# Shared network as eight items of one-pass products, expert outputs parked in gathered rows, router by token tiles

## What is computed

```python
logits = jnp.einsum('bsd,ed->bse', hidden_states, gate_w)
scores = jax.nn.softmax(logits, axis=-1).transpose(0, 2, 1)
topk_w, topk_idx = jax.lax.top_k(scores, cap)
x_tok = jnp.take_along_axis(hidden_states[:, None, :, :], topk_idx[..., None], axis=2)
g = jnp.einsum('becd,efd->becf', x_tok, Wg)
u = jnp.einsum('becd,efd->becf', x_tok, Wu)
h = jax.nn.gelu(g, approximate=False) * u
eo = jnp.einsum('becf,edf->becd', h, Wd) * topk_w[..., None]
flat = flat.at[flat_idx].add(eo.reshape(-1, d))
gs = jnp.einsum('bsd,fd->bsf', hidden_states, Ws_g)
us = jnp.einsum('bsd,fd->bsf', hidden_states, Ws_u)
shared = jnp.einsum('bsf,df->bsd', jax.nn.gelu(gs, approximate=False) * us, Ws_d)
```

## Time and profile before

| what | value |
|---|---|
| median of 3 runs | 706.13 us (705.79 to 706.93) |
| profiled execution | 705.49 us |
| its span, first to last instruction | 703.7 us |
| PE busy | 669.1 us, 95% |
| DVE, ACT, POOL busy | 287.4, 240.2, 34.1 us |
| share of PE in the chain that ended last | 81% |
| granted PE clock, mean | 0.995 |
| expert stage, from the first expert's gate product | 424.8 us on |

### The profile page before, as it was taken

The page is one execution under the profiler, slowest core; times in us unless marked ns, Lnnn a source line. Parts: engine busy times, 40 slices in busy tenths (PEclk is TensorE's granted clock), DMA queues, the critical chain, the costliest instruction groups (busy, mean ns, idle before and its releaser), DMA issues.

```text
span 703.7 us, 10425 instructions
## 1 busy us (share of the span) xinstructions
PE 669.1 (95%) x4272; PEld 427.7 (61%) x4272; DVE 287.4 (41%) x603; ACT 240.2 (34%) x468; POOL 34.1 (5%) x35
## 2 busy tenths in 40 slices
PE   6989999999999999799989789999999999999996
PEld 5767778787777875488966563444444444444532
DVE  5964544636454264766775552111111111111112
ACT  4744545545354452556771131111111111111110
POOL 0300000000000000570000100000000000000000
PEclk9999999999999999999999999999999999999999
DMA  8111011010700000303097704899999999999911
GB/s 306 69 61 61 20 42 61 1 61 2 299 1 2 1 1 2 105 3 129 1 378 278 300 0 141 343 403 373 411 358 391 385 372 383 366 402 373 383 46 61
DMA packets 14348, 129.69 MB, mean 184 GB/s; under 512 B 2720, under 2 KB 2848, under 8 KB 6240
## 3 DMA queue, kind: packets, MB, share of 16 engines
q1 hardware_dynamic: 12384, 127.09, 46.5%
q10 hardware_dynamic: 1920, 1.97, 0.9%
HBM read 126.03 MB, written 1.05 MB: 181 GB/s over the span
## 4 chain that ended last, share of the span: by engine, by line
PE 81%; DVE 10%; ACT 4%; issue 1%; DMA 1%; SPq 1%; ACTq 1%; DVEq 0%
PE ps L969 21%; PE ps L1227 15%; PE ps L1259 8%; PE ps L1234 7%; PE ps L1266 4%; PE ps L1148 4%; PE ps L1039 4%; PE ps L1015 2%; PE ps L1050 2%; PE ps L1248 2%; PE ps L1080 2%; PE ps L1185 2%; PE ps L1197 1%; DVE stats L636 1%; PE ps L1114 1%
## 5 line engine op out<-in xcount | busy, mean ns | idle before, releaser
L865 DVE TENSOR_TENSOR hid<-hid,ps 128x256 f32<-128x256 f32 (+1 forms) x32 | 17.6, 553 | 141.3 <-PE ps L1227 91.4
L579 ACT ACTIVATE hid<-ps 128x256 f32<-128x256 f32 (+1 forms) x32 | 15.7, 490 | 141.6 <-PE ps L1234 86.5
L1259 PE MATMUL ps<-w_d,hid_T 128*64 128x512 f32 x256 | 58.4, 598 | 1.3 <-ACT hid_T L594 1.3
L1227 PE MATMUL ps<-w_u,x_slot 128*64 128x512 f32 x256 | 58.4, 598 | 0.0
L1227 PE MATMUL ps<-w_g,x_slot 128*64 128x512 f32 x256 | 57.8, 594 | 0.0
L465 ACT ACTIVATE probs<-ps,neg_max 128x512 f32<-128x512 f32 x64 | 43.5, 687 | 39.1 <-DVE neg_max L716 39.1
L969 PE MATMUL ps<-wv_hi,ctx_hi 128*128 128x512 f32 x128 | 51.6, 403 | 0.0
L696 DVE COPY probs_T<-ps 128x512 f32<-128x512 f32 x32 | 22.1, 691 | 68.7 <-PE ps L1039 68.7
L969 PE MATMUL ps<-wv_lo,ctx_hi 128*128 128x512 f32 x128 | 50.1, 392 | 0.0
L969 PE MATMUL ps<-wv_hi,ctx_lo 128*128 128x512 f32 x128 | 49.9, 390 | 0.0
L716 DVE TENSOR_REDUCE neg_max<-ps 128x1 f32<-128x512 f32 x64 | 39.7, 683 | 18.4 <-PE ps L1015 18.3
(11 more groups left out here) (192 smaller groups left out, 1145.8 us busy)
## 6 DMA issues: line engine op xcount, KB each, us to landing
w_u<-in_wu SPq DMA_DIRECT2D x16, 2048.0 KB, 15.9
w_d<-in_wd SPq DMA_DIRECT2D x16, 2048.0 KB, 13.9
w_g<-in_wg SPq DMA_DIRECT2D x16, 2048.0 KB, 9.6
ctx_raw<-in_ctx SPq DMA_DIRECT2D x7, 1024.0 KB, 4.7
w_qkv<-in_wqkv SPq DMA_DIRECT2D x1, 3072.0 KB, 15.2
ws_g<-in_wsg SPq DMA_DIRECT2D x1, 2048.0 KB, 7.9
ws_u<-in_wsu SPq DMA_DIRECT2D x1, 2048.0 KB, 8.0
ws_d<-in_wsd SPq DMA_DIRECT2D x1, 2048.0 KB, 21.3
```

The source lines that it names most:

```text
L865: dve.tensor_tensor(hid[:, n % 2, 0:w], hid[:, n % 2, 0:w], ps[:, 2 * (n % 2) + 1, 0:w], ALU.mult).then_inc(hid_done, 1)
L1227: ins = pe.matmul(ps[64 * fh:64 * (fh + 1), dst, :], x_slot[:, dt, e, :], weights[e % 2][:, dt, BANK * fh:BANK * (fh + 1)], start=(dt == 0 ...
L1259: ins = pe.matmul(ps[64 * fh:64 * (fh + 1), 6 + n % 2, :], hid_T[:, n % 2, j, 64 * fh:64 * (fh + 1)], w_d[e % 2][:, KT * fh + j, :], start ...
```

## The change

**Shared network.** Instead of 16 quarters there are eight items. Item i has 128 of the hidden columns and all 512 tokens. Weights, normalised rows and hidden rows are each split in a high part in the one-pass form and the rest, and a product is the sum of three one-pass products (high by high, high by low, low by high). Gate and value products come out as [hidden, token], so no transposes follow; the down products go tile by tile over two pairs of banks. `shared_high_gu`, `shared_high_d` (ScalarE) and `shared_low_gu`, `shared_low_d`, `hidden_low` (VectorE) make the parts. One item stands ahead of the experts, one after each of the experts 1, 3, ... 13.

**Outputs.** `eo_slot` now lies over the shared gate weights, so the rows of batch b can be written only after shared item b. Experts' outputs are parked in their gathered rows in `x_slot`, and `send` puts out what has come free.

**Layer norm and router.** Transposes and copies go by token tiles; VectorE's part (`xn_low_tile`) for tile t-1 stands in the middle of tile t's norm. The router's products have three one-pass parts of 32 columns.

**Start of the stage.** The routing tables lie in the second `w_d` buffer, so the load of w_d for expert 1 waits for their last reader. The broadcast of the scores moves behind the second expert's value product.

```diff
+        eo_slot = sb(first, "eo_slot", [P, B, D])
...
+        ws_g_lo = sb(first, "ws_g_lo", [P, NF, KT, P], F32R)
+        ws_u_lo = sb(first, "ws_u_lo", [P, NF, KT, P], F32R)
...
+        ws_g = sb(moe, "ws_g", [P, NF, KT, P])
+        ws_u = sb(moe, "ws_u", [P, NF, KT, P])
...
-        x_slot = sb(moe, "x_slot", [P, KT, E, SLOTS])
+        x_slot = sb(moe, "x_slot", [P, E, KT, SLOTS])
...
-        SHARED = [("s", t, q * QUARTER, QUARTER) for t in range(NT) for q in range(4)]
-        ITEMS, REST = SHARED[:2], SHARED[2:]
+        SHARED = [("s", i) for i in range(NF)]
+        ITEMS, REST = SHARED[:1], SHARED[1:]
         for e in range(E):
             ITEMS.append(("e", e))
-            for _ in range(2 if e == E - 3 else 1 if 0 < e < E - 3 else 0):
+            if e % 2 and REST:
                 ITEMS.append(REST.pop(0))
         AT = {item: n for n, item in enumerate(ITEMS)}
...
+        def experts_upto(n):
+            return n + 1 - shared_before(n + 1)
+
+        def downs_upto(n):
+
+            return experts_upto(n) + NT * shared_before(n + 1)
+
+        def shared_down_bank(n, t):
+            return (4, 6)[t % 2] + n % 2
...
-            for kind in "gud":
-                expert_load(kind, 1)
+            expert_load("g", 1)
+            expert_load("u", 1)
             for e in range(2, E, 2):
-                for kind, ahead in (("g", 0), ("u", 0), ("g", 1), ("d", 0), ("u", 1), ("d", 1)):
+                for kind, ahead in (("g", 0), ("u", 0), ("g", 1)):
+                    expert_load(kind, e + ahead)
+                if e == 2:
+                    sp.wait_ge(give_ps, 2)
+                    sp.wait_ge(last_T_done, NT)
+                    expert_load("d", 1)
+                for kind, ahead in (("d", 0), ("u", 1), ("d", 1)):
                     expert_load(kind, e + ahead)
...
+            def shared_high_gu(i):
+
+                if i:
+                    act.wait_ge(g_ps, AT["s", i - 1] + 1)
+                    act.wait_ge(u_ps, AT["s", i - 1] + 1)
+                act.copy(ws_g_hi[:], ws_g[:, i]).then_inc(ws_hi_done, 1)
+                act.copy(ws_u_hi[:], ws_u[:, i]).then_inc(ws_hi_done, 1)
+
+            def shared_high_d(i):
+                if i:
+                    act.wait_ge(down_ps, downs_upto(AT["s", i - 1]))
+                act.copy(ws_d_hi[:], ws_d[:, i, :]).then_inc(ws_hi_done, 1)
+
...
+            for t in range(NT):
+                ln_std(2, (t,))
+                if t:
+                    xn_high_tile(t - 1)
+            xn_high_tile(NT - 1)
...
             def send(n):
...
+                ready, free = experts_upto(n - 1), shared_before(n + 1)
+                was_ready, was_free = experts_upto(n - 2), shared_before(n)
+                for e in range(ready):
+                    if e >= was_ready:
+                        act.wait_ge(eo_done, e + 1)
+                    for b in range(0 if e >= was_ready else was_free, free):
+                        row = SLOTS * (e % 2) + CAP * b
+                        act.dma_start(eo_slot[CAP * e:CAP * (e + 1), b, :], eo_of(e)[row:row + CAP, :]).then_inc(eo_sent[e % 2], 16)
...
+                if is_expert(n):
+                    act.wait_ge(hidT_ps, experts_upto(n))
+                    act.copy(hid_T[:, n % 2].rearrange("p j c -> p (j c)"), bank(4 + n % 2)).then_inc(hidT_done, 1)
+                else:
+                    act.wait_ge(hid_done, n + 1)
+                    act.copy(hid_hi[:, n % 2, :], hid[:, n % 2, :]).then_inc(hid_hi_done, 1)
+                if 1 < n < LAST:
+                    send(n)
...
-                elif ITEMS[n][0] == "e":
+                elif is_expert(n):
                     e = ITEMS[n][1]
-                    act.wait_ge(down_ps, n + 1)
-                    if e >= 2:
-                        act.wait_ge(eo_sent[e % 2], 16 * B * (e // 2))
+                    act.wait_ge(down_ps, downs_upto(n))
                     mine, other = eo_rows(e)
-                    act.copy(eo[mine, :], ps[other, 6 + n % 2, :]).then_inc(half_done, 1)
+                    act.copy(eo_of(e)[mine, :], ps[other, 6 + n % 2, :]).then_inc(half_done, 1)
...
+                earlier = ITEMS[n - 2]
+                split_next = earlier[0] == "s" and earlier[1] + 1 < NF
+                if split_next:
+                    shared_high_gu(earlier[1] + 1)
                 item_out(n - 1)
+                if split_next:
+                    shared_high_d(earlier[1] + 1)
             item_out(LAST - 1)
-            send(LAST - 1)
+            send(LAST)
...
+                    if behind and t:
+                        behind(t - 1)
                     ln_rows(k, t, xn)
...
+                if behind:
+                    behind(NT - 1)
+
+            def xn_low_tile(t):
+                toks = slice(P * t, P * (t + 1))
+                dve.wait_ge(xn_hi_done, 2 * KT + t + 1)
+                dve.tensor_tensor(xn_lo_moe[:, :, toks], bank(t).rearrange("p (k c) -> p k c", k=KT),
+                                  xn_hi[:, :, toks].bitcast(F32), ALU.subtract).then_inc(xn_split, 1)
...
+            dve.tensor_tensor(gate_lo[:], gate[:], gate_hi[:].bitcast(F32), ALU.subtract).then_inc(gate_split, 1)
+            shared_low_gu(0)
+            shared_low_d(0)
+            residual_ln(2, xn_moe, xn_low_tile)
...
+            def hidden_low(n):
+
+                dve.wait_ge(hid_hi_done, shared_before(n) + 1)
+                dve.tensor_tensor(hid_lo[:, n % 2, :], hid[:, n % 2, :], hid_hi[:, n % 2, :].bitcast(F32),
+                                  ALU.subtract).then_inc(hid_split, 1)
...
+                        dve.wait_ge(sx_done, NT * shared_before(n))
+                    for t in range(NT):
+                        dve.wait_ge(down_ps, downs_upto(n) - NT + t + 1)
+                        dve.tensor_tensor(x[:, t, :], bank(shared_down_bank(n, t)), x[:, t, :], ALU.add).then_inc(sx_done, 1)
...
+            for n in range(3, LAST):
+                if not is_expert(n - 1):
+                    hidden_low(n - 1)
+                earlier = ITEMS[n - 2]
+                split_next = earlier[0] == "s" and earlier[1] + 1 < NF
+                if split_next:
+                    shared_low_gu(earlier[1] + 1)
                 item_hidden(n)
                 item_sum(n - 1)
+                if split_next:
+                    shared_low_d(earlier[1] + 1)
...
+            def moe_transpose(t):
+                pe.wait_ge(xn_done, 2 * NT + t + 1)
+                for dt in range(KT):
+                    ins = pe.transpose(ps[:, t, P * dt:P * (dt + 1)], xn_moe[:, t, P * dt:P * (dt + 1)], ident[:])
+                ins.then_inc(xnT_ps, 1)
+
...
+            for t in range(NT):
+                moe_transpose(t)
...
+                    i = ITEMS[n][1]
+                    hi, lo = shared_parts
+                    pe.wait_ge(ws_split, 3 * i + off + 1)
+                    for dt in steps:
+                        w_hi_part, w_lo_part = hi[:, dt, :], lo[:, i, dt, :]
+                        for j, (a, c) in enumerate(((w_hi_part, xn_hi), (w_hi_part, xn_lo_moe), (w_lo_part, xn_hi))):
+                            ins = pe.matmul(bank(dst), a, c[:, dt, :], start=(dt == 0 and j == 0),
+                                            stop=(dt == KT - 1 and j == 2))
...
+                    i = ITEMS[n][1]
+                    pe.wait_ge(ws_split, 3 * i + 3)
+                    pe.wait_ge(hid_split, shared_before(n) + 1)
+                    for t in range(NT):
+                        if t >= 2:
+                            pe.wait_ge(sx_done, NT * shared_before(n) + t - 1)
+                        rows = slice(P * t, P * (t + 1))
+                        for j, (a, c) in enumerate(((hid_hi, ws_d_hi[:]), (hid_lo, ws_d_hi[:]), (hid_hi, ws_d_lo[:, i, :]))):
+                            ins = pe.matmul(bank(shared_down_bank(n, t)), a[:, n % 2, rows], c, start=(j == 0), stop=(j == 2))
+                        ins.then_inc(down_ps, 1)
...
             for t in range(NT):
+                toks = slice(P * t, P * (t + 1))
+                pe.wait_ge(xn_split, 2 * KT + t + 1)
                 for dt in range(KT):
-                    ins = pe.matmul(ps[:, 6, LGW * t:LGW * (t + 1)], xn_T[:, dt, P * t:P * (t + 1)], gate[:, dt, :],
-                                    start=(dt == 0), stop=(dt == KT - 1))
+                    for j, (a, c) in enumerate(((xn_hi, gate_hi), (xn_hi, gate_lo), (xn_lo_moe, gate_hi))):
+                        ins = pe.matmul(ps[:, 6, LGW * t:LGW * (t + 1)], a[:, dt, toks], c[:, dt, :],
+                                        start=(dt == 0 and j == 0), stop=(dt == KT - 1 and j == 2))
             ins.then_inc(logit_ps, 1)
-            item_gate(0)
+            item_gate(0, range(2))
             pe.wait_ge(score_done, 1)
             for t in range(NT):
                 ins = pe.transpose(ps[0:E, 7, P * t:P * (t + 1)], logit[:, t, :], ident[:])
             ins.then_inc(scoreT_ps, 1)
+            item_gate(0, range(2, KT))
...
```

(14 more changed lines are left out.)

209 lines of the change are left out of this document (105 added, 104 removed).

## The result

| | kernel before | changed kernel |
|---|---|---|
| median of 4 runs each, side by side | 705.97 us (705.79 to 706.93) | 714.50 us (713.81 to 714.85) |
| ratio | | 1.0117, 95% interval 1.0104 to 1.0130 |
| profiled execution, its span | 705.49, 703.7 us | 714.17, 712.4 us |
| PE busy | 669.1 us | 661.5 us |
| granted PE clock, mean | 0.995 | 0.971 |

The change makes the kernel slower by 1.2%. I had forecast 704.2 us; the time is 10.3 us above that and 1.5 us above the upper end of the range. PE is busy for 7.6 us less and the span is 8.7 us longer; the waits are longer and part of the busy time is at the slower clock. The loss is in two places: the head, up to the first expert (+15.0 us), and the end, behind expert 14's gate product (+9.3).

The account below looks back on a forecast made before the run. TensorE was taken as the bound, weights close behind. 703.7 + 7.5 + 1.9 - 24.9 - 1.0 + 0.7 + 0.75 + 3.3 + 8.3 + 1.7 = 701.9 us of span, +2.4 to the median: 704.2 us, range 697.5 to 713.

Parts of the forecast that it names:

- norm: Last layer norm: VectorE's subtraction for tile 0 waits for late TensorE transposes; last row tile at 406.5, not 397.5, +9.0 us.
- router, to its last product: Router: 48 small products after the last transposes, 5.3 us plus 1.9 for half clock plus 0.44, together 7.6, or +0.3.
- selection to first expert: After the router: slot products start earlier, -0.8 us; first gate waits for the last copy, score broadcast moved behind, -1.0.
- shared items, 36 products each: Expert stage: one-pass products without transposes, 8.19 us an item, replace the quarters; -24.9 us from the first expert gate on.
- `w_d` of expert 1: Early expert stage: this load waits for the routing tables in its buffer and lands at 464.1; TensorE waits +0.75 us.
- late weight loads: Expert stage: loads at 5.39 us each beside sends; w_u of expert 13 lands at 636.6, wanted at 633.2, +3.3 us.
- burst of 21 sends: ScalarE issues them for 13.9 us before copying expert 14's transposed rows; TensorE idle 9.0 us instead of 0.68, +8.3.
- half clock behind it: After the idle time ahead of expert 14's down product, TensorE runs at 1.2 GHz for 3.4 us: +1.7, from 0 to 3.4.
- The -0.8 for slot products: After selection: slot products start when the pick rows end, 415.05, not after a shared product at 415.82, -0.8 us.
- the bank wait: Shared items: each item's third down product waits 0.1 us for its bank to be added, +0.7 in all.
- Rival C: Expert stage: weights become the bound at w_u of expert 13, kernel slower; 5.65 us a load gives 712.6 us; chance 0.22.
- rival D: ScalarE's issue slows with many sends queued, 1.23 us rather than 0.63; last burst costs 12 us more, 716; chance 0.10.

Follow-up runs that it names:

- the first experiment: Changed kernel with each row tile's transposes issued right after the next tile's output-projection products, instead of after all 16: 709.28 us, 1.0039 times the kernel before.
- third experiment: Changed kernel with the four results of a shared item's down products sent to four different banks: 711.07 us, 1.0057 times the kernel before.
- the combined kernel: Changed kernel with interleaved transposes, router products per tile, four banks, 128-partition broadcast, last burst and half of expert 14's sends on SyncE: 695.85 us, 0.9845.

## Why the prediction was wrong

The sum gave a span of 701.9 us; it was 712.4.

| term of the sum | expected | measured | what shows it |
|---|---|---|---|
| half clock near 290 us | 0 | +1.4 | output products from 381.3 instead of 379.9 |
| norm | +9.0 | +8.4 | last rows at 407.3 instead of 397.5, less the row above |
| router, to its last product | +0.3 | +3.9 | 11.2 us instead of 7.3 |
| selection to first expert | -1.8 | +1.3 | 21.3 us instead of 20.0 |
| shared items, 36 products each | 8.29 us each | 9.27 | seven items, +6.9 |
| `w_d` of expert 1 | +0.75 | +1.4 | idle time ahead of its product |
| late weight loads | +3.3 | 0 | no idle time ended by one |
| burst of 21 sends | +8.3 | +6.9 | 7.53 us idle instead of 0.68 |
| half clock behind it | +1.7 | +1.5 | 5.14 against 3.65 |

The first four rows make the first expert 7.5 us later than the 432.3 of the prediction (439.81). From there on the errors add up to +2.7, and the rest took 3.0 us more than forecast (272.6 against 269.6); 0.3 is not assigned.

**Half clock in the head: the step that failed.** "I take 0.11 each, the load of the weights, so 5.3, plus 1.9 for half clock after a thin stretch as before, plus 0.44: 7.6, or +0.3." The stretch took 11.2 us, all of it at half clock. The bound of the whole at half clock was in the text (5.3 + 0.44 + 5.3), and I took the old 3.4 us as the nearest row. It wasn't: those were four-pass products of 96 columns, the new ones are one-pass of 32. The runs with surplus products show both halves: the norm's waits let the clock fall, and with the waits filled it fell in the 32-column products. Why the old router brought the clock back and the new one, even at 96 columns, doesn't, stays open; their form, four passes against one, is the plainest difference left, and it was not tried. The size of the term was also taken for the router alone. The same stretch slowed the last transposes (1.12 for 0.44), the shared products ahead of the scores (2.75) and, in a second fall of its own, the slot products (+1.8). The -0.8 for slot products that no longer wait for a shared product left out what the thinner broadcast in front of them does to the clock: the runs with 128 partitions give back 1.9 and 2.9 us.

**Norm: right.** The block was there, for the reason given; the first experiment takes away 5.3 us of the 8.4. The rest is the pace: 4.45 us a tile instead of 3.44, where I had 4.8, since copy and subtraction add 1.0 and not 1.4.

**Shared items: mechanism right, mis-sized.** This term missed by as much as the head (+6.9 us), and the late weights that didn't come hid half of it. I had 0.228 us from product to product and 2.73 for twelve. In this stage they start every 0.233; each group's first step, and the last one of the value and the down group, cost 0.08 to 0.1 more; and the bank wait, expected as 0.1 an item, was 0.43 in all with its restart (third experiment). Together 0.98 an item. The saving was there: -15.6 us up to expert 14. What slows the steps from 0.228 to 0.233 I didn't test.

**Weights: wrong, in my favour.** The one load that PE waited for is the one behind the routing tables (in brackets the wait):

```profile
473.38 3.65 PE L1376 MATMUL ps<-w_d,hid_T 128*64 128x512 f32 x16 [1.41 <-DMA w_d<-in_wd]
```

The loads took about what I had put in (4.9 us alone, up to 6.1 with sends, 5.32 in the mean of the 32 behind this one against my 5.39), but PE wanted them 1 us per pair later than I had it, since its own items were longer. Rival C, the weights as the bound, is refuted for this kernel. The 358 GB/s that the Trainium skill gives as the limit of a core's loads ("DMA: Bandwidth & Descriptors", section "Where 436 GB/s comes from") doesn't hold for this program on one core, as 425 was reached again without sends. In the combined kernel PE comes to expert 14 some 15 us earlier, and there the weights do arrive just too late.

**Sends: right** in place and mechanism, and the 0.66 for each holds for 21 as for eight, so rival D is wrong. The idle time is 1.5 us shorter than forecast (7.5 instead of 9.0): 0.6 because PE's work ahead of it is longer (7.3 us instead of 6.7), and 0.9 because the first send went out during the GELU and the copy was ready 14.8 us after expert 14's gate instead of 15.7.

**What to have seen.** The forecast bounded each unknown cost and then took a value below the middle for the clock. The upper end, 3.4 us more in the router, was in the text; it gives 707.6 instead of 704.2. With half clock on what stands around it too, sized by what was measured here (0.7 for the transposes, 1.3 for the shared products, 1.8 for the slot products), an estimate in hindsight is 711.

## To carry to other kernels

Where an edit makes a long product into many small ones, cost it at both clock levels, and ask of the work around it whether it can bring the clock back: it is the whole thin stretch that slows down, not the small products alone. An engine's queue is in order, so a burst of transfers or a subtraction put ahead of another engine's input costs its length, less the work that the other engine has left (13.9 us of sends cost 6.9 of idle time here); moving its place, not its number, was worth 5 to 6 us here twice. And a wait that is removed at one place is followed to the next: 3.5 of 8.4 us came back at the final products.

## What the runs showed of the hardware

- One-pass products that follow each other without a gap, with weights of 128 columns and 32 moving columns, ran at 1.2 GHz for 10 us; at full clock the clock fell 3.6 us after the first of them. With 96 columns a full clock stayed full in the one profile of that run, and one at half stayed at half.
- Behind two four-pass products over 16 partitions the clock was at half for 3.4 or 6.8 us in ten profiles; behind the same products over 128 partitions it stayed full in seven.
- At half clock such a product starts every 0.213 us, at full clock every 0.11, whether it has 32 or 96 columns.
- The same code had a stretch of half clock of 3.4 us, 6.8 us or none at one place in different executions; what follows it started at 377.8 to 381.3 us, up to 3.5 us that no edit explains.
- A small transfer took 0.51 us to issue on GpSimd, 0.66 on ScalarE and 0.67 on SyncE. The last send landed 2.0 us after its issue in the changed kernel, 3.7 with the last burst on SyncE, and 8.0 in the combined kernel, with 25 sends of SyncE issued before it and a 2 MB load in flight.
